# One block instead of two for a decoder layer's two attentions, with work moved across the former seam

## What is computed

```python
x = x + linear_attention(layernorm(x))      # 32 heads of 128, silu on q, k, v, decays, rms norm, sigmoid gate, out projection
x = x + cross_attention(layernorm(x), ctx)  # q and k from ctx, v from x; softmax over 512, batches of 64 x 512
x = x + layernorm(x) @ identity.T           # identity is a 512 x 512 input
```

## Time and profile before

| | |
|---|---|
| median of 3 runs | 2140.43 us (2138.98 to 2140.65) |
| the profiled execution, own time | 2140.66 us |
| its span, first to last instruction | 2138.8 us (1.86 us lie around it) |
| mean TensorE clock of the span | 0.994 |
| DVE, ACT, POOL busy | 65%, 53%, 36% of the span |
| second block begins | 1846.2 us into the span |

### The profile page before, as it was taken

The page is one execution under the profiler, slowest core; times in us unless marked ns, Lnnn a source line. Parts: engine busy times, 40 slices in busy tenths (PEclk is TensorE's granted clock), DMA queues, the critical chain, the costliest instruction groups (busy, mean ns, idle before and its releaser), DMA issues. The chain is left out here.

```text
span 2138.8 us, 42516 instructions
## 1 busy us (share of the span) xinstructions
PE 2084.2 (97%) x16208; PEld 1704.1 (80%) x16208; DVE 1398.8 (65%) x1992; ACT 1129.1 (53%) x1927; POOL 762.5 (36%) x882
## 2 busy tenths in 40 slices
PE   6999999999999999999999999999999999799998
PEld 5788888888888888888888888888888887466665
DVE  6666666565656667766666656666665655688885
ACT  4545455554545455555555545455555544566664
POOL 6344334252525343534343343344342522211110
PEclk9999999999999999999999999999999999899999
DMA  3111211111111120202111111111111112301110
GB/s 123 54 57 42 61 40 57 44 50 50 50 47 54 39 61 31 63 21 61 42 61 41 50 50 40 60 40 60 40 51 50 50 51 58 105 30 54 51 36 20
DMA packets 40502, 109.49 MB, mean 51 GB/s; under 512 B 4960, under 2 KB 9568, under 8 KB 40288
## 3 DMA queue, kind: packets, MB, share of 16 engines
q1 hardware_dynamic: 40128, 107.25, 15.9%
q10 hardware_dynamic: 288, 1.05, 0.1%
HBM read 104.09 MB, written 4.19 MB: 51 GB/s over the span
## 5 line engine op out<-in xcount | busy, mean ns | idle before, releaser
L482 POOL TENSOR_TENSOR raw<-raw 128x256 f32<-128x256 f32 x128 | 129.5, 1012 | 600.0 <-DMA raw<-w_pairs 600.0
L1015 PE MATMUL bank<-x_hi,w_hi_c 128*128 128x512 f32 x672 | 267.1, 397 | 2.1 <-DVE v L803 1.5
L1020 PE MATMUL bank<-x_hi,w_lo_c 128*128 128x512 f32 x672 | 262.2, 390 | 0.0
L1018 PE MATMUL bank<-x_lo,w_hi_c 128*128 128x512 f32 x672 | 261.7, 389 | 0.0
L1072 PE MATMUL bank<-wo_hi,y_hi 128*128 128x512 f32 x512 | 205.3, 401 | 4.1 <-DVE y_lo L841 3.1
L1073 PE MATMUL bank<-wo_lo,y_hi 128*128 128x512 f32 x512 | 202.5, 395 | 0.0
L1074 PE MATMUL bank<-wo_hi,y_lo 128*128 128x512 f32 x512 | 202.2, 395 | 0.0
L513 POOL TENSOR_TENSOR sq_acc<-sq_acc,sq 128x512 f32<-128x512 f32 x124 | 160.3, 1293 | 88.9 <-ACT sq L677 79.7
L803 DVE TENSOR_TENSOR qk<-bank,qk 128x512 f32<-128x512 f32 x192 | 127.3, 688 | 85.2 <-ACT qk L648 42.6
L1015 PE MATMUL bank<-x_hi,w_hi_a 128*128 128x512 f32 x448 | 176.2, 393 | 0.0
L1020 PE MATMUL bank<-x_hi,w_lo_a 128*128 128x512 f32 x448 | 175.0, 391 | 0.0
(11 more groups left out here) (157 smaller groups left out, 5480.2 us busy)
## 6 DMA issues: line engine op xcount, KB each, us to landing
raw<-w_pairs SPq DMA_DIRECT2D x126, 512.0 KB, 3.6
raw<-w_out SPq DMA_DIRECT2D x32, 512.0 KB, 3.6
xr<-x SPq DMA_DIRECT2D x4, 1024.0 KB, 7.3
raw<-ctx_in SPq DMA_DIRECT2D x16, 256.0 KB, 3.0
raw<-ctx_in SPq DMA_DIRECT2D x32, 128.0 KB, 3.1
out<-attn_acc SPq DMA_DIRECT2D x16, 256.0 KB, 2.0
attn_acc<-x SPq DMA_DIRECT2D x8, 256.0 KB, 6.1
decays<-decay SPq DMA_DIRECT2D x32, 64.0 KB, 3.0
```

The lines of the kernel that those rows point to most:

```text
L482: nc.gpsimd.tensor_tensor(raw[:, S1], raw[:, S3], raw[:, A22], ALU.add).then_inc(done, 1)
L1015: nc.tensor.matmul(bank[:, to], w_hi[w][:, a, s], x_hi[:, b, c], start=part in ("first", "only") and c == 0, stop=False, skip_group_check= ...
L1018: nc.tensor.matmul(bank[:, to], w_hi[w][:, a, s], x_lo[:, b, c], start=False, stop=False, skip_group_check=True)
L1020: i = nc.tensor.matmul(bank[:, to], w_lo[w][:, a, s], x_hi[:, b, c], start=False, stop=part in ("last", "only") and c == 1, skip_group_che ...
```

## The change

The two functions no longer open blocks. Each returns five functions, one per engine, and `decoder_layer` runs both of an engine in one block, one behind the other. The bodies move one level to the left; apart from that only these lines differ (`...` marks what is left out):

```diff
+Programs = namedtuple("Programs", "sync gpsimd scalar vector tensor")
...
-        attention(nc, sb, sem, bank, attn_acc, sq_acc, ident, ones, cross, x, w_pairs, w_out, norm_w, decay, ident_in)
-        cross_and_ffn(nc, sb, sem, bank, attn_acc, ident, cross, out)
+        first = attention(nc, sb, sem, bank, attn_acc, sq_acc, ident, ones, cross, x, w_pairs, w_out, norm_w, decay,
+                          ident_in)
+        second = cross_and_ffn(nc, sb, sem, bank, attn_acc, ident, cross, out)
+
+        with nc.Block() as block:
+
+            @block.sync
+            def _(sp):
+                first.sync(sp)
+                second.sync(sp)
...
+            @block.tensor
+            def _(pe):
+                first.tensor(pe)
+                second.tensor(pe)
```

VectorE in the first part, the mean squares and the last tiles:

```diff
                 weighted(half, d, 0)
+                if not following:
+                    cross.mean_squares(dve, 0, 7)
                 project(half, d, QK2, lambda: cut_a(half, d, 2, 0))
...
                 add_out(half, d, 0, 0)
-                    if not following:
-                        cross.mean_squares(dve, 0, 7)
...
                     cross.q_low(dve, 0, 4)
-                        for j in range(CH):
-                            add_out(half, d, 1, j)
-                            if j == 2:
-                                y_low(half, d, 1, 1)
-                            cross.row_max(dve, 0, j, early_pair[j % 2])
+                    for i in range(2):
+                        add_out(half, d, 1, i)
+                    cross.row_max(dve, 0, 0, early_pair[0])
+                    for i in range(2, TT):
+                        add_out(half, d, 1, i)
+                    y_low(half, d, 1, 1)
+                    cross.row_max(dve, 0, 1, early_pair[1])
+                    cross.row_max(dve, 0, 2, early_pair[0])
                     cross.make_x1(dve, 1)
-                        for i in range(TT, HT):
+                    for i in range(TT, TT + 2):
+                        add_out(half, d, 1, i)
+                    cross.row_max(dve, 0, 3, early_pair[1])
+                    for i in range(TT + 2, HT):
                         add_out(half, d, 1, i)
                     cross.k_low(dve, 1, 3)
```

TensorE, the last tiles, and waits in place of the meeting:

```diff
                     cross.scores(pe, 0, 0, early_pair[0])
-                        rest_out(half, d, 1, (2,))
+                    rest_out(half, d, 1, (2, 3))
                     cross.scores(pe, 0, 1, early_pair[1])
-                        rest_out(half, d, 1, (3,))
                     pe.wait_ge(cross.S["exp_ready"], 2)
                     cross.scores(pe, 0, 2, early_pair[0])
-                        rest_out(half, d, 1, (4,))
+                    rest_out(half, d, 1, (4, 5))
                     pe.wait_ge(cross.S["exp_ready"], 4)
                     cross.scores(pe, 0, 3, early_pair[1])
-                        rest_out(half, d, 1, (5, 6, 7))
+                    rest_out(half, d, 1, (6, 7))
                     pe.wait_ge(cross.S["exp_ready"], 6)
                     cross.project_qk(pe, 1, 2, 3)
                     pe.wait_ge(out_added, count(half, d, 16, 14))
                     cross.values(pe, 0, 1)
                     sums(1, 0)
+                    pe.wait_ge(out_added, 2 * QUADS * 16)
...
                     if t >= 2:
                         pe.wait_ge(S["out_ready"], t - 1)
+                    elif t == 0:
+                        pe.wait_ge(S["k_ready"], 2)
+                        pe.wait_ge(S["q_ready"], 2)
                     cross.project_qk(pe, t + 2, MISC, KEYS)
```

ScalarE and VectorE in the second part, the parts of `eye` (all four stood at the end of pair 0):

```diff
                 keep_turned(t, 1)
                 if t:
                     cross.normed(act, 3, 1, t - 1, xn3[:, :])
+                else:
+                    for c in range(0, 2):
+                        eye_high(c)
...
                     xn3_high(t - 1)
+                else:
+                    for c in range(2, CH):
+                        eye_high(c)
                 keep_turned(t, 3)
...
                 keep_turned(t, 2)
+                if t == 1:
+                    for c in range(2, CH):
+                        eye_low(c)
                 if t + 1 < PAIRS:
                     cross.keep_values(dve, t + 1, MISC)
                     cross.row_max(dve, t + 1, 2, FIRST)
                 keep_turned(t, 3)
                 if t:
                     xn3_low(t - 1)
+                else:
+                    for c in range(0, 2):
+                        eye_low(c)
```

More of the change, by code:

```diff
@@ L7 @@
+from collections import namedtuple
 from contextlib import ExitStack
@@ L238, in decoder_layer, with _ @@
                           eye_in, (wq_in, wk_in, wv_in, bq_in, bk_in, bv_in))
-        attention(nc, sb, sem, bank, attn_acc, sq_acc, ident, ones, cross, x, w_pairs, w_out, norm_w, decay, ident_in)
-        cross_and_ffn(nc, sb, sem, bank, attn_acc, ident, cross, out)
+        first = attention(nc, sb, sem, bank, attn_acc, sq_acc, ident, ones, cross, x, w_pairs, w_out, norm_w, decay,
[6 more added lines that the diff above has]
+                second.sync(sp)
+            @block.gpsimd
+            def _(pool):
+                first.gpsimd(pool)
+                second.gpsimd(pool)
+            @block.scalar
+            def _(act):
+                first.scalar(act)
+                second.scalar(act)
+            @block.vector
+            def _(dve):
+                first.vector(dve)
+                second.vector(dve)
+            @block.tensor
+            def _(pe):
+                first.tensor(pe)
+                second.tensor(pe)
 def attention(nc, sb, sem, bank, attn_acc, sq_acc, ident, ones, cross, x, w_pairs, w_out, norm_w, decay, ident_in):
@@ L1222, in cross_and_ffn @@
+        return Programs(sync, gpsimd, scalar, vector, tensor)
 def cross_and_ffn(nc, sb, sem, bank, x1, ident, cross, out):
@@ new lines, in sync @@
+        def sync(sp):
+            for t in range(PAIRS):
+                if t + 2 < PAIRS:
+                    sp.wait_ge(S["qk_mm"], t + 1)
+                    cross.load_ctx(sp, t + 2)
+                if t >= 2:
+                    sp.wait_ge(S["out_ready"], t - 1)
+                    sp.dma_start(out_t[t - 2], x1[:, t - 2]).then_inc(S["stored"], 16)
+            for t in range(PAIRS - 2, PAIRS):
+                sp.wait_ge(S["out_ready"], t + 1)
+                sp.dma_start(out_t[t], x1[:, t]).then_inc(S["stored"], 16)
+            sp.wait_ge(S["stored"], 16 * PAIRS)
```

1910 lines of the change are left out of this document (940 added, 970 removed).

## The result

| | before | changed |
|---|---|---|
| median (runs) | 2140.12 us (4, 2138.98 to 2140.65) | 2122.68 us (4, 2120.42 to 2124.95) |
| ratio of the two | | 0.9919, 95% interval 0.9902 to 0.9936 |
| profiled execution, own time | 2140.66 us | 2124.95 us |
| its span | 2138.8 us | 2123.1 us |

The change is 17.4 us faster (medians); 18.1 were forecast, for 2122.6 us. The profiled execution is the slowest of its four, and the times of the changed kernel spread over 4.5 us where those of before spread over 1.7. Both are part of what follows.

What follows compares the result with a forecast made beforehand. TensorE, busy 97% of the span, was taken as the bound, losing time only to waits and low clock. Gains of 21.0 us less 2.95 of new waits gave 18.1, from 2140.66 to 2122.6 us; range 2119.5 to 2126.0.

Steps and rivals of the forecast that it cites:

- A: Mean squares of the first half, moved earlier: 3.1 us wait for GpSimd and 1.7 of low clock go, gain 4.8.
- B: New order of the last output tiles: shorter wait before tile 4 (0.7) and fewer changes (0.4), gain 1.1 us.
- C: Meeting of the two blocks, between the second sums and pair 0: TensorE's pause goes, gain 4.9 us.
- D: Context load of pair 2, issued earlier by SyncE: TensorE's wait for it goes, gain 2.9 us.
- E: Low clock after the seam, in the first transposes, projections and 1852 to 1857 us, goes: gain 3.4 us.
- G (1): New wait in pair 0 for ScalarE's first copy, held up by normalising pair 1: 1.1 us lost.
- G: New waits in pairs 0 and 1: 1.1, then 0.9 and 1.8 (1.25 of it added), then 0.6; loss 2.95 us.
- F: Parts of `eye` moved from before pair 1's copy: 2.3 us wait and 1.6 of low clock go, gain 3.9.
- R1: Rival: the clock falls again after the new waits in pair 0, costing 1.6 us, 2124.2 in all; chance 0.23.
- R2: Rival: 2.4 us of the seam's pause is code arriving late and stays, 2125.5 us in all; chance 0.10.
- R3: Rival: merging makes the first part's loop turns stop for code, up to 29 us, 2151 in all; chance 0.02.

Runs made afterwards that it cites:

- the plain two blocks: The changed kernel with only the merging undone, so two blocks with a meeting of the engines between them; 2131.41 us, ratio 0.9963.
- the best one: The changed kernel with ScalarE's normalisation of pair 1 moved later and the parts of `eye` put where their engines idle; 2118.01 us, ratio 0.9894.

## Why the prediction was right, and where only its sum was

**A, B and C are confirmed** to 0.1 us each, by the cuts of the two traces and by undoing A and B alone (4.7 and 1.08 us). GpSimd's quarter of QK2 stood behind a small power that VectorE fed late; one instruction of 0.15 us, moved by 9 us, was worth 4.7.

**D and E are confirmed as one**: the seam cost 10.4 us in the traces (4.8 of pause and 5.6 behind it), where C, D and E less G (1) said 10.1.

**G is confirmed** in its first two entries (waits of 1.09, 0.93 and 1.58 us for 1.1, 0.9 and 1.8). The 0.6 us of the third were 0.4, a wait for ScalarE's copy, and 0.2 more for the values where the clock held.

**What failed in its size is the clock in F.** The step said of the 2.3 us wait and its low clock, 1.6 us: "Both go". The wait went; the low clock moved. The new waits before pair 1 are followed by a fall in six of the nine profiled executions that have them (both of the changed kernel among them), and in the changed kernel it costs 2.7 us (38.42 and 38.47 us from pair 0 to pair 2, against 35.73). So putting `eye` back changes nothing in the median, where 2.0 us were expected. That was rival R1, given a chance of 0.23 and a price of 1.6; it is the more frequent case, at 2.7.

**Why the number still came out.** The sum was made against a profiled execution of before that had the low clock in the last pair (last transposes to last matmul 14.7 us, 12.5 where the clock holds), and it carried those 2.2 us on without saying so. Its reading that TensorE runs without a stop from pair 2 on hid this: in the last two pairs there are waits of 0.9, 0.9, 0.4, 1.9 and 1.4 us, the same in both kernels. The forecast without any fall is therefore 2120.4, which is what the one execution at a mean clock of 1.000 took. Both profiled executions of the changed kernel have the fall before pair 1, 2.7 us, and part of the one in the last pair, 1.6 us (14.1 us there), and took 2124.6 and 2125.0; the median lies between them and the case without any. Two errors, of 2.2 and up to 2.7 us and with opposite signs, are hidden in the agreement with 2122.68; that it is within 0.1 us is luck.

**R2 was half right.** The pause of 4.9 us was not a meeting: that takes 0.3. GpSimd's way from its last instruction into it took 3.1 to 3.3, with a packet of code in the pause. In the merged kernel nobody waits for that, so nothing of it stays. The Trainium skill (Runtime: NRT & Kernel Launch, Instruction fetch mechanics) has a stall wherever a taken branch leaves the code at hand; by that rule it would be GpSimd's jump out of its first program, and the packet in the pause agrees. That the packets come behind GpSimd's last instruction wherever that lies speaks for it too. What is not shown is that GpSimd stood still for them; what fills the 3.1 us stays open.

**R3** did not occur: pair 2 to pair 15 is unchanged, and TensorE's only wait for issue in the span is 0.2 us (0.4 in the earlier trace rows).

## What to carry to other kernels

Cut two traces at the same instructions before reading medians: edits worth 1.1 us were plain there and invisible in executions that spread over 4 us. When a wait goes, ask where the next idle time of TensorE lies and how long it is: making it 1.2 us longer cost 4.0 in the same stretch, and filling idle places of the side engines so that only short waits were left won 5.0 us over the change. A meeting of engines costs as much as the slowest way into it, and whatever is loaded behind it.

## What the runs showed that I had not expected

The same waits are followed by a low clock in one profiled execution and not in another. These are executions of different versions: the changed kernel itself was profiled twice, and fell both times before pair 1. Before pair 1, waits of 0.93 and 1.58 us a microsecond apart were followed by it in six of nine traces; waits of 1.87 and 1.41 us in the last pair in ten of fourteen (not in the plain two blocks, in the versions with the mean squares or `eye` back, and in the best one, which all kept 12.5 us from the last transposes to the last matmul). One wait of 1.41 us never was; one of 2.62 us was. The two places together, 2.7 and 2.2 us, are as large as the spread of 4.5 us. The nine mean clocks of the changed kernel follow the times, as far as three decimals tell: 1.000 at 2120.42, 0.999 at 2122.18 and 2122.58, 0.998 at 2122.78 to 2123.03 and once at 2124.71, 0.997 at 2124.61 and 2124.95.

In the one trace where GpSimd had been done long before, a meeting of the five engines took 0.33 us from the last instruction to TensorE's next.
